# Reordering a cross-attention and mixture-of-experts kernel: keys stacked ahead of queries, new orders in the ramp, half of the late places on ScalarE, the last step's second weights first

## The reference

```python
q, k, v = LN(x) @ Wq.T + bq, ctx @ Wk.T + bk, ctx @ Wv.T + bv   # 16 heads of 16, B=16, S=112, C=375, D=256
p = softmax(where(mask == 0, -1e9, q k.T / 4))
x = x + (p v) @ Wo.T + bo
t = LN(x).reshape(1792, 256)
g = softmax(t @ router_w); take the two best of 8, their weights made to sum to 1 (cw)
y[e] = silu(t @ w1[e]) @ w2[e]                                   # 256 -> 512 -> 256
out = x + sum over e of y[e] * cw[:, e]
```

## Time and profile before

| what | us |
|---|---|
| median of 3 runs | 467.08 (467.06 to 467.87) |
| the profiled execution's own time | 465.15 |
| its span | 463.3 |
| PE busy | 414.2 (89% of the span) |
| DVE busy | 340.2 (73%) |
| ACT busy | 277.9 (60%) |
| POOL busy | 224.4 (48%) |

### The profile page before, as it was taken

How to read it: one execution, slowest core, us unless ns; L and a number is a source line. 1 busy time by engine, 2 the same in 40 slices (tenths; PEclk the granted TensorE clock), 3 DMA queues, 4 the chain that set the end, 5 groups by cost and what they waited for, 6 DMA issues and landing times.

```text
span 463.3 us, 10813 instructions
## 1 busy us (share of the span) xinstructions
PE 414.2 (89%) x4219; PEld 385.6 (83%) x4219; DVE 340.2 (73%) x699; ACT 277.9 (60%) x374; POOL 224.4 (48%) x254
## 2 busy tenths in 40 slices
PE   7867899999998999999999997589989999999810
PEld 6746798998897998899998996579989999999810
DVE  7965677887787877788878868966686676777545
ACT  4547655656665566656554553447777777778600
POOL 6754642024431344421312573755787787876420
PEclk9888999999999999999999998579999999999975
DMA  7794527774768766667660149922222222332169
GB/s 209 190 214 128 133 73 157 154 185 117 170 146 180 163 143 154 147 139 151 131 129 11 48 150 373 317 59 70 80 81 84 88 91 81 92 82 69 45 224 296
DMA packets 50692, 64.32 MB, mean 139 GB/s; under 512 B 18834, under 2 KB 39587, under 8 KB 50643
## 3 DMA queue, kind: packets, MB, share of 16 engines
q1 hardware_dynamic: 44338, 50.40, 43.4%
q0 software_dynamic: 4096, 11.13, 8.2%
q10 hardware_dynamic: 2208, 2.12, 1.4%
HBM read 30.13 MB, written 9.28 MB: 85 GB/s over the span
## 4 chain that ended last, share of the span: by engine, by line
PE 76%; DVE 8%; DMA 6%; issue 3%; ACT 3%; SPq 1%; POOL 1%; ACTq 0%; POOLq 0%; DVEq 0%
PE ps L1533 39%; PE ps L1596 12%; PE ps L1613 9%; PE ps L1627 9%; DMA k_stack<-k_lo 2%; PE ps L1900 2%; PE ps L1640 2%; DMA mask_scratch<-mask_rows 1%; DMA y_rows<-y_out,slot_of_row 1%; DMA y_back<-y_rows 1%; DVE neg_max L1095 1%; PE ps L1696 1%; DMA keep_scratch<-keep_all 1%; PE ps L1652 1%; DMA mask_all<-mask 1%
## 5 line engine op out<-in xcount | busy, mean ns | idle before, releaser
L1095 DVE TENSOR_REDUCE neg_max<-ps 112x1 f32<-112x376 f32 x256 | 133.6, 545 | 45.2 <-PE ps L1596 40.5
L829 ACT ACTIVATE probs<-ps 125x1344 f32<-125x1344 f32 x64 | 82.7, 1293 | 43.8 <-PE ps L1613 38.6
L1596 PE MATMUL ps<-k_stack,q_stack 98*112 98x376 f32 x256 | 86.6, 372 | 8.1 <-issue 3.6
L602 POOL TENSOR_TENSOR k_lo<-k_f,k_hi 128x752 fp32r<-128x752 f32 x16 | 28.9, 1808 | 118.0 <-ACT k_hi L803 118.0
L760 POOL DMA_INDIRECT rows<-xn_rows,token_of_row x42 | 55.2, 1315 | 18.9 <-issue 12.5
L1596 PEld LDWEIGHTS ps<-k_stack,q_stack 98*112 98x112 f32 x256 | 44.8, 177 | 21.0 <-DVE neg_max L1095 10.6
L768 POOL DMA_INDIRECT y_rows<-y_out,slot_of_row x42 | 47.3, 1126 | 25.8 <-ACT y_out L1022 14.5
L1613 PE MATMUL ps<-q_stack,k_stack 100*125 100x224 f32 x384 | 52.5, 272 | 0.0
L1613 PEld LDWEIGHTS ps<-q_stack,k_stack 100*125 100x125 f32 x384 | 50.6, 188 | 0.6 <-ACT probs L829 0.5
L1533 PE MATMUL ps<-w_hi,h_hi 128*128 128x256 f32 x168 | 48.7, 290 | 1.6 <-issue 1.6
L1533 PE MATMUL ps<-flat_t_hi,w_hi 128*128 128x256 f32 x168 | 47.5, 283 | 1.9 <-DVE flat_t_lo L1420 1.9
(11 more groups left out here) (213 smaller groups left out, 1024.8 us busy)
## 6 DMA issues: line engine op xcount, KB each, us to landing
k_stack<-k_hi SPq DMA_DIRECT2D x32, 376.0 KB, 5.8
w_all<-w SPq DMA_DIRECT2D x2, 4096.0 KB, 18.9
k_stack<-k_lo SPq DMA_DIRECT2D x16, 376.0 KB, 7.1
ctx_raw<-ctx_t SPq DMA_DIRECT2D x32, 187.5 KB, 6.4
q_stack<-attn_t_hi SPq DMA_DIRECT2D x64, 56.0 KB
y_back<-y_rows SPq DMA_DIRECT2D x14, 256.0 KB, 4.7
x_rows_sb<-x_rows SPq DMA_DIRECT2D x4, 448.0 KB, 5.1
x<-x_tiles SPq DMA_DIRECT2D x7, 256.0 KB, 3.8
```

The source lines that it names most:

```text
L602: pool.tensor_tensor(kl[:, :, :], kf[:, :, :], kh[:, :, :].bitcast(F32), ALU.subtract)\
L829: act.activation(pf[j % 2][:, :, :], ps[0:CT, BK_ST:BK_ST + KT, 0:4 * S], ACT.Exp).then_inc(pf_ready, 1)
L1095: dve.tensor_reduce(neg_max[:, s:s + 1], ps[0:S, BK_MAX + s % 2, 0:CP], AX.X, ALU.max, negate=True).then_inc(max_read, 1)
L1596: pe.matmul(ps[0:S, BK_MAX + a, 0:CP], qs[b.ring][0:R_MAX, q, S * a:S * (a + 1)], ks[b.ring][0:R_MAX, q, :], start=True, stop=True).then_i ...
```

## The change

- **Layout of the queries.** The tiles `attn_t_hi` and `attn_t_lo`, which hold the queries until the attention's output takes their place, keep both halves of a batch's queries next to each other, and the query stack is ordered `[2, HALF, S]` instead of `[HALF, 2 S]`: a run of a query DMA's source is 224 numbers instead of 112 and the target's rows are contiguous. The second scores' moving operand becomes two runs of 112; the maxima are written in the new order of heads; `query_low` and `first_query_low` become two instructions for one.
- **SP's turn.** `stack_keys`, then `stack_queries`, then `stack_mask` (before: queries, mask, keys), after a wait that the second scores of batch b-1 are done.
- **SP in the ramp.** The mask rows go to DRAM before two loads; keys and queries of batch 0 are stacked before its mask; `load_rows(3)` and the context of batch 2 go behind the query stack, and the latter behind the key stack too, of batch 1.
- **Lists in the ramp.** ACT: the output projection's weights and the router's before `normalise_x(2)` and `key_high` of batch 1; `q_high(1, 0)` before `x_std(3)` and the table load; `q_high(1, 1)` before `normalise_x(3)`. DVE: the scaling of `bq_c` before `attn_weight_low(1)`. POOL: `key_low` of batch 2 before `query_low(3)` instead of after it.
- **Late places.** ACT makes `is_place` of the late tiles for choice 1, DVE for choice 0; DVE's lanes come in reverse order, and PE waits for each lane by itself.
- **Last expert step.** `w2_high` comes before `silu`, and `w2_low` before `h_low`, in the last step only.

```diff
-        qh = [th[:, :, SG * g:SG * (g + 1)] for g in range(NG)]
-        ql = [tl[:, :, SG * g:SG * (g + 1)] for g in range(NG)]
+        qh, ql = (x.rearrange("p a (b k n) -> p b a k n", k=KD, n=S) for x in (th, tl))
...
-        qs = [sb(f"q_stack{p}", [P, HALF, 2 * S], F32R) for p in range(RINGS - 1)]
+        qs = [sb(f"q_stack{p}", [P, 2, HALF, S], F32R) for p in range(RINGS - 1)]
...
-                queue.dma_start(qs[b.ring][row + c:row + PARTS * DK:PARTS, :, S * a:S * (a + 1)].bitcast(F32),
-                             src[half:half + P // 2, :, S * b.n:S * (b.n + 1)].bitcast(F32))\
-                    .then_inc(done, 16)
+                queue.dma_start(qs[b.ring][row + c:row + PARTS * DK:PARTS, a, :, :].bitcast(F32),
+                                src[half:half + P // 2, b.n // 2, b.n % 2, :, :].bitcast(F32)).then_inc(done, 16)
...
             def stack_queries(b):
-                if not early(b, RINGS):
-                    sp.wait_ge(st_done, QUADS * (b.n - RINGS + 1))
...
             def turn(b):
                 if has(b.after(2)):
-                    stack_queries(b.after(2))
                     if b.n == 0:
                         sp.wait_ge(xt_done, NG)
+                    else:
+                        sp.wait_ge(st_done, QUADS * b.n)
+                    stack_keys(b.after(2))
+                    stack_queries(b.after(2))
                     stack_mask(b.after(2))
-                    stack_keys(b.after(2))
...
             load_keep(0, slice(0, 2))
+            sp.wait_ge(mask_rows_ready, 1)
+            sp.dma_start(mask_scratch, m_rows[:, :, :].bitcast(F32)).then_inc(mask_written, 16)
             load_weight(2, wv_t)
             load_rows(2)
-            sp.wait_ge(mask_rows_ready, 1)
-            sp.dma_start(mask_scratch, m_rows[:, :, :].bitcast(F32)).then_inc(mask_written, 16)
             load_weight(3, wo_t)
             sp.dma_start(rw_raw[:, :, :], router_w.rearrange("k p n -> p k n")).then_inc(rw_in, 16)
+            stack_keys(first)
+            stack_queries(first)
             sp.wait_ge(mask_written, 32)
             stack_mask(first)
-            stack_keys(first)
-            stack_queries(first)
-            load_rows(3)
-            load_ctx(first.after(2))
             sp.wait_ge(filled, 4)
             stack_queries(second)
             stack_mask(second)
+            load_rows(3)
             stack_keys(second)
+            load_ctx(first.after(2))
             load_ctx(first.after(3))
...
             query_low(2)
+            key_low(first.after(2))
             query_low(3)
...
-                if has(b.after(2)):
+                if has(b.after(2)) and b.n:
                     key_low(b.after(2))
...
             x_std(2)
-            normalise_x(2)
-            key_high(second)
             attn_weight(3)
             act.wait_ge(rw_in, 16)
             act.copy(rw[:, :, 0:E], rw_raw[:, :, :]).then_inc(rw_ready, 1)
+            normalise_x(2)
+            key_high(second)
             x_high(2)
             values(first, True)
             values(first, False)
+            q_high(1, 0)
             x_std(3)
             act.activation(root_c[:, :], eps_c[:, :], ACT.Exp)
-            q_high(1, 0)
+            q_high(1, 1)
             normalise_x(3)
-            q_high(1, 1)
...
             for k, c in enumerate((1, 0)):
-                early_places_in_block(k, c)
+                places_in_block(k, c, slice(0, EARLY_NT))
+            places_in_block(TOP, 1, slice(EARLY_NT, NT))
...
             def step(t):
+                final = is_step(t) and not is_step(t.after(1))
+                if final:
+                    w2_high(t)
                 if is_step(t):
                     silu(t)
...
-                    dve.tensor_reduce(neg_max[:, s:s + 1], ps[0:S, BK_MAX + s % 2, 0:CP], AX.X, ALU.max,
+                    head = HALF * (s % 2) + s // 2
+                    dve.tensor_reduce(neg_max[:, head:head + 1], ps[0:S, BK_MAX + s % 2, 0:CP], AX.X, ALU.max,
...
-                for c, n in lanes_of(part)[POOL_LANES[part]:]:
+                for c, n in reversed(lanes_of(part)[POOL_LANES[part]:]):
...
             def expert_step(t):
                 if is_step(t.after(1)):
                     rows_low(t.after(1))
+                final = is_step(t) and not is_step(t.after(1))
+                if final:
+                    w2_low(t)
                 if is_step(t):
                     h_low(t)
+                if is_step(t) and not final:
                     w2_low(t)
...
-            for c in range(TOP):
-                late_places_in_block(c)
+            late_places_in_block()
...
-                                         qs[b.ring][0:ROWS, 2 * j + q, :], start=True, stop=True)
+                                         qs[b.ring][0:ROWS, :, 2 * j + q, :], start=True, stop=True)
...
-                pe.wait_ge((early_places, late_places)[part], TOP)
-                pe.wait_ge(dve_lanes, dve_before + len(on_dve))
+                pe.wait_ge(scalar_places, TOP + part)
                 for a, (c, n) in enumerate(on_dve):
+                    pe.wait_ge(dve_lanes, dve_before + a + 1)
+                    if part == 1 and c == 0 and on_dve[a - 1][0] == 1:
+                        pe.wait_ge(late_places, 1)
                     last = fill(c, n, part == 0 and a == 0, False)
```

More of the change, by code:

```diff
@@ L620, in query_low @@
                 pool.wait_ge(qh_ready, KD * (g + 1))
-                pool.tensor_tensor(ql[g], qf[:, :, :], qh[g].bitcast(F32), ALU.subtract)\
-                    .then_inc(ql_ready, 1)
-            fills = [(qs[0][R_MASK:ROWS, :, :], 1.0), (vx[0][:, :, :, DK:VC], 1.0),
-                     (qs[1][0:R_MASK, :, :], 0.0), (qs[1][R_MASK:ROWS, :, :], 1.0), (vx[1][:, :, :, DK:VC], 1.0),
-                     (qs[2][0:R_MASK, :, :], 0.0), (qs[2][R_MASK:ROWS, :, :], 1.0)]
+                for b in range(2):
+                    last = pool.tensor_tensor(ql[:, 2 * g + b, :, :, :], qf[:, b, :, :, :],
+                                              qh[:, 2 * g + b, :, :, :].bitcast(F32), ALU.subtract)
+                last.then_inc(ql_ready, 1)
+            fills = [(qs[0][R_MASK:ROWS, :, :, :], 1.0), (vx[0][:, :, :, DK:VC], 1.0),
+                     (qs[1][0:R_MASK, :, :, :], 0.0), (qs[1][R_MASK:ROWS, :, :, :], 1.0), (vx[1][:, :, :, DK:VC], 1.0),
+                     (qs[2][0:R_MASK, :, :, :], 0.0), (qs[2][R_MASK:ROWS, :, :, :], 1.0)]
             assert len(fills) == N_FILLS
@@ L644, in _ @@
             pool.wait_ge(ql_ready, 1)
-            stack_part(pool, first, 1, tl, first_low_stacked)
+            stack_part(pool, first, 1, ql, first_low_stacked)
             fill(range(1, 5))
@@ L958, in _, with places_in_block @@
                 flat_high(u)
-            def early_places_in_block(k, c):
-                if k == 0:
-                    act.wait_ge(in_block_known, 1)
-                if c == 0:
+            def places_in_block(k, c, tiles):
+                act.wait_ge(in_block_known, 1 if k < TOP else 2)
+                if k < TOP and c == 0:
                     for p in range(RINGS, XN_RINGS):
                         act.wait_ge(xn_written[p], 16)
-                for n in range(EARLY_NT):
+                for n in range(tiles.start, tiles.stop):
                     last = act.activation(is_place[:, c, n, :], place_no, ACT.Abs,
@@ L971, in early_places_in_block @@
                 act.wait_ge(distances_set, k + 1)
-                act.activation(is_place[:, c, 0:EARLY_NT, :], is_place[:, c, 0:EARLY_NT, :].bitcast(F32), ACT.Relu,
-                               bias=1.0, scale=-1.0).then_inc(early_places, 1)
+                act.activation(is_place[:, c, tiles, :], is_place[:, c, tiles, :].bitcast(F32), ACT.Relu,
+                               bias=1.0, scale=-1.0).then_inc(scalar_places, 1)
             for k, c in enumerate((1, 0)):
-                early_places_in_block(k, c)
+                places_in_block(k, c, slice(0, EARLY_NT))
+            places_in_block(TOP, 1, slice(EARLY_NT, NT))
             def rows_high(t):
@@ L1159, in first_query_low @@
                 dve.wait_ge(qh_ready, t + 1)
-                ins = dve.scalar_tensor_tensor(out=ql[0][:, t, :], in0=ps[:, (2, BK_OUT)[t], 0:SG],
-                                               scalar=bq_c[:, t:t + 1], in1=qh[0][:, t, :].bitcast(F32),
-                                               op0=ALU.add, op1=ALU.subtract)
+                for b in range(2):
+                    ins = dve.scalar_tensor_tensor(out=ql[:, b, :, t, :], in0=pairs(ps[:, (2, BK_OUT)[t], 0:SG])[:, b, :, :],
+                                                   scalar=bq_c[:, t:t + 1], in1=qh[:, b, :, t, :].bitcast(F32),
+                                                   op0=ALU.add, op1=ALU.subtract)
                 if t == KD - 1:
@@ L1595, in head_scores @@
                     a, q = s % 2, s // 2
-                    pe.matmul(ps[0:S, BK_MAX + a, 0:CP], qs[b.ring][0:R_MAX, q, S * a:S * (a + 1)],
```

(1 more changed line is left out.)

47 lines of the change are left out of this document (24 added, 23 removed).

## The result

The changed kernel takes 456.43 us (median of 4 runs, 455.64 to 457.65) against 467.07 for the kernel before beside it: ratio 0.9773, 95% interval 0.9747 to 0.9799. It is 10.6 us faster, where 7.55 were forecast; 456.43 lies just outside the range's low end of 456.9. The profiled execution took 456.5 us, its span 454.4.

A forecast was written before the change was run, and what follows sets the result against it. The prediction took PE, busy for 89% of the span, as the bound. Terms 4.0 + 0.7 + 0.6 + 1.35 + 0.9 = 7.55 us, off the median 467.08, gave 459.5 us; the 8-in-10 range was 456.9 to 463.2.

The forecast's parts named there:

- the ramp's 0.7: Ramp up to the ninth maximum: it starts at 37.35 instead of 38.03, a gain of 0.7 us, between 1.6 and -1.9.
- Last step: Last expert step: second weights made ahead let the last output product start 1.15 us sooner; gain 0.9, between 0.4 and 1.15.
- DVE's adds cap the gain: End of the kernel: DVE's adds, eighth at 449.38, would end at 458.3 against 459.25 now, limiting the gain to 0.9.
- At nothing: Changes taken as 0 us: longer query DMA runs, scaling of `bq_c`, split `first_query_low`, two-run operand of the second scores.
- Keys first: Attention turns 1 to 13: keys issued ahead of queries end PE's wait for the last key DMA; gain 4.0 us.
- Rival 3: Attention turns: queries land last and PE waits, 463.5 us; chance 0.08 without gain, 0.03 slower.
- the new wait: Ramp: `x_stats(3)` on DVE waits for the late load of x's fourth group, taken to need 4.7 us, landing at 33.0.
- Rival 1: Ramp: the late load of x lands with the first bound, at 32.1, giving 458.6 us; chance 0.20.
- Turn 0: First attention turn: of PE's 0.91 us idle before batch 3's first key matmul, 0.6 is won, between 0.2 and 0.9.
- Late places: Routing: PE's late fills start at 298.5 instead of 299.93; gain taken as 1.35 us, between 0.9 and 1.45.
- rival 4: Second scores in attention: the two-run operand slows each by 10 ns, giving 463.3 us; chance 0.04.
- the gap of 1.93 us: Whole kernel before: the median of runs lay 1.93 us above the profiled 465.15, so the sum was taken off 467.08.

## Why the prediction was wrong

The direction was right, and so were the terms for the keys, turn 0 and the late places. Two steps fail and make the forecast too small by 1.7 to 2.0 and by 1.3 us, about the miss of 3.07 us (459.5 - 456.43). A third, the ramp's 0.7, fails the other way.

- **Last step: the term of 0.9 is mis-sized; it is 2.6 alone and 2.9 undone.** "DVE's adds cap the gain" took the start of that run of adds at 449.38 as fixed, as though only DVE's own work stood ahead of it. It was not DVE that held it but a load back, as its row says (0.69 us idle for `y_back`), and the loads had the last write among them. With `w2` first the last write leaves 1.2 us sooner, behind three loads instead of four, and lands 2.0 us faster; the second choice's loads then come before DVE wants them. The 1.15 us ahead of the product were right (1.60 - 0.42 = 1.18).
- **"At nothing": the scaling of `bq_c` was not free; its move is worth 1.3 us in the trace, 0.9 to 1.3 by the medians.** I named the cover on DVE's own list (its 4.13 us of idleness) and did not look at who waits for what stands behind the scaling: the first keys, through them ACT, the low queries, POOL's fills and SP's issue of the late load. Nor did I read its 1.74 us as a wait. That it was one for POOL's instruction is shown by 1.74 against 0.16 us at the same place. The Trainium skill ("SBUF — State Buffer", section "SBUF: two separate sides") says that DVE and GpSimd share a pair of ports, which a GpSimd instruction, or a DVE one in a two-port mode or with two inputs in SBUF, holds for its whole length while the other waits. The trace agrees: in the kernel before the scaling ends at 13.52 and POOL's instruction at 13.49.

The others:

- *Keys first:* 4.0 forecast; 4.06 alone, 3.81 in turns 1 to 12 (168.67 - 164.86). Right, with the cause as named. Of the 0.64 us put down to matmuls that restart only 0.18 went (PE's busy time in the twelve turns is 165.04 before, 164.86 after): a turn without a wait takes 13.74 us on the mean, not 13.70. Rival 3, queries last, appears only where `k_lo` is made late (turn 0 with `key_low` put back).
- *Ramp:* the new wait and its 4.7 us are right; the gain of 0.7 is not. From the load's landing to the ninth maximum it took 4.76 us (4.35 forecast). That maximum came at 36.71 (37.35 forecast), but 1.27 us of that are the scaling's: with the scaling back it comes at 37.98, and 38.03 before. So the orders win about nothing up to there: all of what the earlier ones bring is given back to the late load, and that the number came out near the forecast is luck. Rival 1's landing time, 32.1, was met (31.95), by an earlier issue and not by a faster load.
- *Turn 0:* 0.6 forecast, 0.55 measured (14.21 to 13.66). Of the 0.91 us of idle time ahead of the key matmul 0.32 are left, where the prediction took none as a sign of being right.
- *Late places:* 1.35 forecast; 1.64 and 1.38 against the two profiles of before, 1.5 with the part undone. The late fills do start with ACT's Relu.
- *Second scores:* 273 ns against 272; rival 4 did not come.
- *The end of the sum:* the gap of 1.93 us between profile and median did not persist (456.5 and 456.43): the first profile of before was one of the shorter executions of a kernel that ran from 464.5 to 471.4 us. Taking the sum off the median was right all the same.

Measured one by one: 4.06 (keys) + 2.62 (last step) + 1.27 (scaling) + 1.5 (late places) + 0.55 (turn 0) = 10.0 of 10.64 us. These are medians and stretches of different runs, so that they add up this well is in part luck. The rest may lie in the ramp's orders, or in PE's wait for the next rows in the fifth step (1.39 before, 0.75 after); neither was tried alone, and at this spread it could hardly be told.

The late load of x took 4.7 us with queries and a mask ahead of it and a key stack right behind: 0.9 more than the quiet one and 2.6 less than the one with a key stack ahead. Whether the 0.9 us come from the key stack behind or from the queries ahead, no run shows. The Trainium skill ("DMA: Bandwidth & Descriptors", section "Queues, rings and completion order") says that a DMA engine takes the descriptors of a ring in order. The trace agrees in that the load with more ahead of it landed later; the quiet time alone was too short.

## What to carry to other kernels

For an instruction costed at nothing, follow what stands behind it through all lists to the next DMA that another list waits for; idle time further down its own list is no cover. Where a late write to DRAM must land before further loads may start, as at the end of this kernel, a write that leaves with fewer loads ahead of it is worth more than its own lead. When an order is changed so that a list waits earlier, make what it waits for earlier too, or the list carries the delay to all that is behind it.

## What the hardware showed

- A DVE instruction of 2 elements in each partition took 1.74 us while POOL subtracted 752 (1.81 us), and 0.15 to 0.16 us without it; another, of 4 elements, took 1.58 beside the same POOL instruction and 0.16 without. Not every DVE instruction waits so: the two that make `k_f`, with one input in PSUM, take 1.13 us in the changed kernel, where POOL's instruction lies over them, and 1.13 with it moved away.
- The same write to DRAM landed 6.3 us behind its issue with four loads ahead of it and more behind, 4.3 with three ahead and more behind, and 3.6 with three ahead and the others held.
- The routing of the same kernel took 64.68 us at a granted clock of 0.84 and 65.70 at 0.79 (1.2 GHz for 20.5 and for 27.3 us of it); turns 1 to 12, at 2.4 GHz throughout, took 168.67 and 168.41.
